# fp4 feed-forward: fp16 halves split in SBUF and turned by DMA transposes instead of TensorE transposes

## The reference

```
x = x + 0.5 * L0_ffn(layernorm(x));  x = x + L0_attn(layernorm(x));  x = x + 0.5 * L0_ffn(layernorm(x))
x = x + 0.5 * L1_ffn(x);             x = x + L1_attn(layernorm(x));  x = x + 0.5 * L1_ffn(x)
```

```
def fp4_quant_dequant(x):               # blocks of 16 along the last dim
    scale = maximum(max(abs(xb)) / 6, 1e-12)
    return GRID[searchsorted(MID, abs(xb / scale))] * sign(xb) * scale      # GRID = 0 .5 1 1.5 2 3 4 6
def fp4_linear(x, w): return einsum('bsk,nk->bsn', fp4_quant_dequant(x), fp4_quant_dequant(w))
h = silu(fp4_linear(x, w_gate)) * fp4_linear(x, w_up)                       # w: (704, 256)
return fp4_linear(h, w_down)                                                # w_down: (256, 704)
```

## Time and profile before

| | us |
|---|---|
| median of three runs | 2584.41 |
| span of the profiled execution, the only time that the page gives for it | 2581.7 |
| PE busy | 2337.3 |
| DVE busy | 1892.3 |
| ACT busy | 1681.8 |
| POOL busy | 880.3 |

### The profile page before, as it was taken

How to read it: one execution, slowest core, us unless ns; L and a number is a source line. 1 busy time by engine, 2 the same in 40 slices (tenths; PEclk the granted TensorE clock), 3 DMA queues, 4 the chain that set the end, 5 groups by cost and what they waited for, 6 DMA issues and landing times.

```text
span 2581.7 us, 54517 instructions
## 1 busy us (share of the span) xinstructions
PE 2337.3 (91%) x22748; PEld 1779.9 (69%) x22748; DVE 1892.3 (73%) x3201; ACT 1681.8 (65%) x2940; POOL 880.3 (34%) x631
## 2 busy tenths in 40 slices
PE   2889989888999998999898989989898989999999
PEld 2556666666777776777676767667676768777788
DVE  8788889997896887777878777668777774542631
ACT  4476666555757684776757575757767586675666
POOL 1222122212413221363536344453626264132122
PEclk9899999998999998999999999999999999999999
DMA  5000000000000000000000000000000000000000
GB/s 177 19 1 1 1 1 1 1 1 1 1 1 1 1 1 26 2 18 10 14 14 14 14 4 24 2 26 2 14 22 14 22 2 10 9 1 9 9 10 9
DMA packets 34981, 33.08 MB, mean 13 GB/s; under 512 B 7664, under 2 KB 34096, under 8 KB 34736
## 3 DMA queue, kind: packets, MB, share of 16 engines
q1 hardware_dynamic: 34736, 29.60, 3.5%
HBM read 12.54 MB, written 4.19 MB: 6 GB/s over the span
## 4 chain that ended last, share of the span: by engine, by line
PE 67%; DVE 18%; ACT 7%; issue 4%; POOL 2%; SPq 1%; DMA 1%; DVEq 0%; ACTq 0%
PE psum L747 17%; PE psum L749 16%; PE psum L748 16%; PE psum L753 6%; PE psum L1174 2%; PE psum L1176 2%; PE psum L1025 2%; PE psum L1175 2%; PE psum L1078 2%; DVE a1pr L1939 1%; PE psum L1055 1%; ACT a1PT L1481 1%; DVE a1nm L1916 1%; POOL a1pr L2177 1%; SPq L722 1%
## 5 line engine op out<-in xcount | busy, mean ns | idle before, releaser
L2190 POOL TENSOR_TENSOR f1hT<-f1g,f1hT 128x512 f16<-128x512 f32 x256 | 306.6, 1202 | 641.3 <-ACT f1hT L1584 640.5
L2177 POOL TENSOR_TENSOR a1pr<-a1PT,a1pr 128x1024 f16<-128x1024 f32 (+1 forms) x176 | 360.7, 2051 | 293.4 <-DVE a1pr L1939 293.3
L747 PE MATMUL psum<-f1sl,f1w1h 128*128 128x256 f16 x1024 | 285.1, 278 | 9.8 <-ACT f1g L1579 7.7
L747 PE MATMUL psum<-f1w2h,f1hT 128*128 128x256 f16 x1024 | 281.4, 275 | 6.1 <-issue 3.9
L748 PE MATMUL psum<-f1sl,f1w1h 128*128 128x256 f16 x1024 | 284.6, 278 | 0.0
L749 PE MATMUL psum<-f1sl,f1w1l 128*128 128x256 f16 x1024 | 284.3, 278 | 0.0
L748 PE MATMUL psum<-f1w2l,f1hT 128*128 128x256 f16 x1024 | 280.5, 274 | 0.0
L749 PE MATMUL psum<-f1w2h,f1hT 128*128 128x256 f16 x1024 | 280.4, 274 | 0.0
L1916 DVE TENSOR_REDUCE a1nm<-psum 128x2 f32<-128x768 f32 (+3 forms) x176 | 197.9, 1124 | 59.5 <-PE psum L1005 58.4
L1939 DVE CAST a1pr<-a1PT 128x1024 f16<-128x1024 f32 (+1 forms) x176 | 173.6, 988 | 77.6 <-ACT a1PT L1481 64.0
L2166 POOL TENSOR_TENSOR f0h<-f0Y,f0sc 128x704 f32<-128x704 f32 x64 | 91.4, 1428 | 326.4 <-DVE f0Y L1786 326.3
(11 more groups left out here) (344 smaller groups left out, 6904.1 us busy)
## 6 DMA issues: line engine op xcount, KB each, us to landing
a1Q<-a1st SPq DMA_DIRECT2D x96, 64.0 KB, 2.6
a1K<-a1st SPq DMA_DIRECT2D x96, 64.0 KB, 2.6
x<-in_L_attn_x SPq DMA_DIRECT2D x8, 512.0 KB, 8.0
out<-x SPq DMA_DIRECT2D x8, 512.0 KB, 3.0
wslot<-in_L_ffn_w SPq DMA_DIRECT2D x1, 1024.0 KB, 8.7
wraw<-in_L_ffn_w SPq DMA_DIRECT2D x1, 1024.0 KB, 5.9
wslot<-in_L_ffn_slot_embeds SPq DMA_DIRECT2D x1, 1024.0 KB, 8.2
a1Q<-a1mr SPq DMA_DIRECT2D x64, 4.0 KB, 1.7
```

The lines of the kernel that those rows point to most:

```text
L747: e.matmul(out, lh, rh, start=start, stop=False)
L2177: e.tensor_tensor(a1["pr"][:, i % 2, 1, :, 0:w], a1["PT"][:, i % 2, :, 0:w], a1["pr"][:, i % 2, 0, :, 0:w], ALU.subtract).then_inc(s["a1_pl"])
L2190: e.tensor_tensor(hT1[:, c % 2, 1, 2 * hp:2 * hp + 2, :], gg[:, hp % 2, :, :], hT1[:, c % 2, 0, 2 * hp:2 * hp + 2, :], ALU.subtract).then_ ...
```

## The change

The fp4 feed-forward no longer uses PE to turn its operands.

- The halves are split before turning. For tokens ACT copies f0xh to fp16 and DVE subtracts the low half, one instruction each per pair. For inner values ACT copies f0h to fp16 (704 columns) and POOL subtracts the low half (704 columns); the product L2166 stays on POOL ahead of both. The halves live in the memory of f0Mx and f0M, read as fp16 (names xhl and hhl).
- SP issues DMA transposes from these into f0xT (four per pair of tiles, 128x256 fp16 each, 64 KB) and f0hT (two per tile, 128x768 fp16 each, 192 KB).
- The scaling by XS and HS that sat in the PSUM copies moves into the constants of the scale computation (1/6 becomes XS/6 or HS/6, and so on).
- The last 64 inner values are no longer doubled: the sixth block has them in its first 64 rows, and the weights' rows 64 to 127 of it are set to zero, after a copy of the upper rows to the lower ones.
- Waits follow: Abs into f0Mx and f0M waits for the transposes that read the buffer before, the gate products wait for f0_x0 or f0_x1, the down products for f0_h0 or f0_h1. The planner gets an entry for the transposing DMA, and orders all engines anew.

The diff, without the lists of semaphore names and of generators, the constants of the inner values' scales, and unchanged lines:

```diff
@@ -262,6 +262,9 @@
...
         return self.vec(out)
+
+    def dma_start_transpose(self, out, src):
+        return self.note(60, None, 2.0 * out.shape[0] * self.each(out))
@@ -571,11 +574,14 @@
...
               "scx": sb("f0scx", [P, 2, 2 * D // 16], f32, stA), "xT": sb("f0xT", [P, 2, 2, 2, 2 * P], f16, stA),
-              "h": sb("f0h", [P, 3, F], f32, stA), "Y": sb("f0Y", [P, 2, FC * P], f32, stA), "M": sb("f0M", [P, 2, F], f32, stA),
+              "h": sb("f0h", [P, 3, F], f32, stA), "Y": sb("f0Y", [P, 2, FC * P], f32, stA), "M": sb("f0M", [P, 2, FC * P], f32, stA),
               "sc": sb("f0sc", [P, 2, 2, F // 16], f32, stA), "hT": sb("f0hT", [P, 2, 2, FC * P], f16, stA),
...
+
+        xhl = f0["Mx"][:, :].bitcast(f16).rearrange("p (m i d) -> p m i d", m=2, i=2)
+        hhl = f0["M"][:, :, :].rearrange("p i n -> p (i n)").bitcast(f16).rearrange("p (i n) -> p i n", i=2)
@@ -730,11 +736,35 @@
...
+            def f0_tokens(f):
+                S = at_f0(f)
+                for tp in range(2):
+                    yield S + 7.0 + 20.0 * tp
+                    q.wait_ge("f0_xl", 2 * f + tp + 1)
+                    if f > 0:
+                        q.wait_ge("f0_u", 4 * (f - 1) + 2 * tp + 2)
+                    for i in range(2):
+                        for m in range(2):
+                            e.dma_start_transpose(f0["xT"][:, tp, m, :, i * P:(i + 1) * P], xhl[:, m, i, :]).then_inc(s[f"f0_x{tp}"], 16)
+
+            def f0_hidden(f):
+                S = at_f0(f)
+                for t in range(NT):
+                    ft = 4 * f + t
+                    yield S + 10.0 + 10.0 * t + 14.6
+                    q.wait_ge("w_k", 4)
+                    q.wait_ge("f0_hl", ft + 1)
+                    q.wait_ge("f0_dn", ft - 1)
+                    for m in range(2):
+                        e.dma_start_transpose(f0["hT"][:, t % 2, m, :].rearrange("p (c n) -> p c n", c=FC),
+                                              hhl[:, t % 2, m * F:m * F + FC * P]).then_inc(s[f"f0_h{t % 2}"], 16)
+
             def last():
...
-            return [weights(), *[chain(z, B) for z in (load, a1_moves, store)], last()]
+            return [weights(), *[chain(z, B) for z in (load, a1_moves, store)],
+                    *[chain(z, 2 * B) for z in (f0_tokens, f0_hidden)], last()]
@@ -804,21 +834,6 @@
...
-            def f0_tokens(f):
-                S = at_f0(f)
-                for tp in range(2):
-                    yield S + 7.0 + 20.0 * tp
-                    q.wait_ge("f0_xq", 2 * f + tp + 1)
-                    if f > 0:
-                        q.wait_ge("f0_u", 4 * (f - 1) + 2 * tp + 2)
-                    v = bank(0)
-                    for k in range(2):
-                        for i in range(2):
-                            o = (2 * k + i) * P
-                            ins = tr(v[:, o:o + P], f0["xh"][:, i, k * P:(k + 1) * P])
-                    ins.then_inc(s["f0_xT"])
-                    banks.after(0, "f0_xl", 2 * f + tp + 1)
-
             def f0_gate(f):
@@ -831,8 +846,7 @@
...
                             q.wait_ge("w_l", W_L["tail", 1])
-                            q.wait_ge("f0_xl", 2 * f + t // 2 + 1)
-                            q.wait_ge("f0_hT", 2 * (ft - 2))
+                            q.wait_ge(f"f0_x{t // 2}", 64 * (f + 1))
                         v = bank(n)[:, 0:FH]
@@ -852,22 +866,12 @@
...
                     hT = f0["hT"][:, t % 2, :, :]
-                    for p, cs in enumerate(((0, 1, 2, 3), (4, 5))):
-                        yield G + 14.3 + 0.6 * p
-                        q.wait_ge("f0_hq", ft + 1)
-                        v = bank(2 + p)
-                        for c in cs:
-                            o = min(c * P, F - P)
-                            ins = tr(v[:, (c - 4 * p) * P:(c - 4 * p + 1) * P], f0["h"][:, ft % 3, o:o + P])
-                        ins.then_inc(s["f0_hT"])
-                        banks.after(2 + p, "f0_hl", 2 * ft + p + 1)
                     for c in range(FC):
...
                             yield G + 18.2 + 0.3 * c
-                        if c in (0, 4):
-                            q.wait_ge("w_k", 4)
-                            q.wait_ge("f0_hl", 2 * ft + c // 4 + 1)
                         if c == 0:
+                            q.wait_ge("w_k", 8)
+                            q.wait_ge(f"f0_h{t % 2}", 32 * (ft // 2 + 1))
                             v = bank(2)[:, 0:D]
@@ -1332,17 +1336,17 @@
...
                     q.wait_ge("ln_rs", 2 * (f + 1))
-                    q.wait_ge("f0_xT", n)
+                    q.wait_ge("f0_xl", n)
                     for i in range(2):
...
                     q.wait_ge("f0_xm", n + 1)
+                    q.wait_ge("f0_x1", 64 * f)
+                    q.wait_ge("f0_x0", 64 * (f + tp))
                     e.activation(f0["Mx"][:, :], f0["Yx"][:, :], ACT.Abs, scale=MAGIC).then_inc(s["f0_xr"])
-                    yield S + 7.8 + 20.0 * tp
-                    q.wait_ge("f0_xT", n + 1)
-                    if f > 0:
-                        q.wait_ge("f0_u", 4 * (f - 1) + 2 * tp + 2)
-                    e.activation(f0["xT"][:, tp, 0, :, :], psum[:, 0, :].rearrange("p (k n) -> p k n", k=2), ACT.Copy, scale=XS).then_inc(s["f0_xh"])
+                    yield S + 6.2 + 20.0 * tp
+                    q.wait_ge("f0_xq", n + 1)
+                    e.activation(xhl[:, 0, :, :], f0["xh"][:, :, :], ACT.Copy).then_inc(s["f0_xh"])
@@ -1351,26 +1355,22 @@
...
                     q.wait_ge("f0_g", ft + 1)
-                    if ft >= 3:
-                        q.wait_ge("f0_hT", 2 * (ft - 2))
+                    q.wait_ge("f0_hl", ft - 2)
                     e.activation(f0["h"][:, ft % 3, :].rearrange("p (i n) -> p i n", i=2), psum[:, 0:2, 0:FH], ACT.Silu,
...
                     q.wait_ge("f0_hm", ft + 1)
-                    e.activation(f0["M"][:, t % 2, :], f0["Y"][:, t % 2, 0:F], ACT.Abs, scale=MAGIC).then_inc(s["f0_hr"])
+                    q.wait_ge(f"f0_h{t % 2}", 32 * (ft // 2))
+                    e.activation(f0["M"][:, t % 2, 0:F], f0["Y"][:, t % 2, 0:F], ACT.Abs, scale=MAGIC).then_inc(s["f0_hr"])
...
                     G = S + 10.0 + 10.0 * t
-                    for p in range(2):
-                        cs = slice(4 * P * p, 4 * P * p + (4 * P, 2 * P)[p])
-                        n = cs.stop - cs.start
-                        yield G + 15.3 + 1.2 * p
-                        q.wait_ge("f0_hT", 2 * ft + p + 1)
-                        q.wait_ge("f0_dn", ft - 1)
-                        e.activation(f0["hT"][:, t % 2, 0, cs], psum[:, 2 + p, 0:n], ACT.Copy, scale=HS).then_inc(s["f0_hh"])
+                    yield G + 12.8
+                    q.wait_ge("f0_hq", ft + 1)
+                    e.activation(hhl[:, t % 2, 0:F], f0["h"][:, ft % 3, :], ACT.Copy).then_inc(s["f0_hh"])
@@ -1602,6 +1602,8 @@
...
                 e.tensor_copy(idb[:, :], cst[:, C_ID:C_ID + P]).then_inc(s["w_k"])
+                for i in range(2):
+                    e.memset(hhl[:, i, 2 * F:2 * FC * P], 0.0).then_inc(s["w_k"])
@@ -1648,8 +1650,12 @@
...
                         q.wait_ge("w_l", W_L[key])
-                        e.memset(wd[0][0:64, FC - 1, :], 0.0).then_inc(s["w_k"])
-                        e.memset(wd[1][0:64, FC - 1, :], 0.0).then_inc(s["w_k"])
+                        q.wait_ge("w_k", 4)
+                        for m in range(2):
+                            e.tensor_copy(wd[m][0:64, FC - 1, :], wd[m][64:128, FC - 1, :]).then_inc(s["w_k"])
+                        q.wait_ge("w_k", 6)
+                        for m in range(2):
+                            e.memset(wd[m][64:128, FC - 1, :], 0.0).then_inc(s["w_k"])
@@ -1733,24 +1739,22 @@
...
                     q.wait_ge("f0_xn", 2 * n + 2)
-                    q.wait_ge("f0_xq", n)
+                    q.wait_ge("f0_xl", n)
                     e.tensor_reduce(c_, blocks16(v), AX, ALU.max, apply_absolute_value=True).then_inc(s["dve"])
                     q.wait_ge("dve", q.tick())
-                    e.tensor_scalar(c_, c_, 1.0 / 6.0, 1e-12, ALU.mult, ALU.max).then_inc(s["dve"])
+                    e.tensor_scalar(c_, c_, XS / 6.0, XS * 1e-12, ALU.mult, ALU.max).then_inc(s["dve"])
                     q.wait_ge("dve", q.tick())
...
                     q.wait_ge("dve", q.tick())
-                    e.scalar_tensor_tensor(blocks16(Yx), blocks16(v), -TIE, bc(r_, 16), ALU.mult, ALU.mult).then_inc(s["f0_xm"])
+                    e.scalar_tensor_tensor(blocks16(Yx), blocks16(v), -TIE * XS, bc(r_, 16), ALU.mult, ALU.mult).then_inc(s["f0_xm"])
                     yield S + 4.6 + 20.0 * tp
...
                     e.scalar_tensor_tensor(Yx, Mx, MAGIC, Yx, ALU.max, ALU.subtract).then_inc(s["f0_xy"])
-                    yield S + 8.4 + 20.0 * tp
+                    yield S + 6.6 + 20.0 * tp
                     q.wait_ge("f0_xh", n + 1)
-                    xT = f0["xT"][:, tp, :, :, :]
```

(33 more changed lines are left out.)

## The result

The changed kernel took 2605.7 us (median of four runs, 2604.3 to 2612.9) against 2582.4 of the kernel before on the same chip: a ratio of 1.0092, 95% interval 1.0076 to 1.0107, slower by 0.9%. The forecast was 2560.

The account below looks back on a forecast made before the run. PE's own work was taken as the bound. Span: 2581.7 - 56.3 (transposes) - 13.6 (POOL waits) + 38 (late data) + 8 (start and end) = 2557.8 us; forecast 2560, its own range 2538 to 2586, overall range 2520 to 2720.

Parts of the forecast that it names:

- Bound by PE: Whole kernel: PE's own work sets the end, busy 2337 of 2581.7 us, with handovers to DVE here and there.
- Removed from PE, 56.3 us: Feed-forward on PE: 512 fp32 transposes go, 0.11 us each, all 56.3 us counted as gain.
- Waits for POOL, 13.6 us: PE from 100 to 980 us: its waits for the POOL products vanish, 8.9 and 4.7 us, 13.6 us gained.
- DVE, ACT, POOL without terms: Other engines: DVE net -69.5 us, ACT net -12, POOL +104 hidden as throughput; all counted at nothing.
- The new path, 8.0 us for a tile of inner values: POOL product to first down matmul: 8.0 us, 4.1 us longer, with 4.5 us for the pair of DMAs.
- SP, "about 2.4 us of 14.2": SP's queue: 2 issues per tile and 4 more per pair take about 2.4 us of each 14.2 us tile.
- "The token transposes ... free.": Token DMAs before the gate products: asked for one half f ahead, so free except at start and end.
- the two ends: Token transposes at 55 us and 978 us: no other tile beside them, so 2 x 4 = 8 us lost.
- "I let half of each delay reach PE: 38 us.": Down products: data 1.2 us later than the order assumes, half reaching PE on 64 tiles, 38 us lost.
- The order, no term: All engines' newly planned order: no cost or gain entered in the sum for other work.
- Rival 2: First down matmul of each tile: transposes land late, PE stands there; 204 us lost, 2726 us; chance 0.31.
- Rival 3: DMA stream is the bound: pieces run one after another, 20.8 against 14.2 us per tile, +422 us, 3000 us; chance 0.05.

Follow-up runs that it names:

- a_merge: Changed kernel with one transposing DMA per pair of token tiles and one per tile of inner values, booked at 1250 ns, planned anew: 2514.1 us.
- t_both: Changed kernel in the stored order of the kernel before, with removed pieces taken out and the new ones fitted in: 2919.9 us.
- g_unmerge: Changed kernel's own code, four and two transposing DMAs, in exactly the order of a_merge: 2522.5 us.
- h_cost: Changed kernel with only the inner values by DMA, tokens still turned on PE, planned anew at 1250 ns per transposing DMA: 2573.6 us.
- x_cost: Changed kernel with only the tokens by DMA, inner values still turned on PE, planned anew at 1250 ns per transposing DMA: 2611.4 us.
- t_h: Changed kernel with only the inner values by DMA, tokens still turned on PE, in the adapted order of the kernel before: 2804.0 us.
- t_x: Changed kernel with only the tokens by DMA, inner values still turned on PE, in the adapted order of the kernel before: 2755.3 us.

## Why the prediction was wrong

The sign was wrong, 2560 for 2606; on the spans, 2557.8 for 2603.0, 45.2 us. These 45.2 us are 21.8 that PE did not save (34.5 for 56.3), 18.3 more behind the silu and 30.0 spread over PE's other idle time, less 24.9 by which the waits on the tiles of the change grew less than forecast (7.5 for 38 + 8 - 13.6 = 32.4). So the terms that the forecast had for waiting were too large, not too small; what failed is what it had at nothing. Step by step, in its order:

- **Bound by PE.** Right: 88% of the span is still PE, and the chain is PE 58%.
- **Removed from PE, 56.3 us.** Right as work (62.9 us in a_merge at nearly the clock of before), 34.5 us in the changed kernel, with a granted clock of 0.955 for 0.971 and PE's idle time at 300 for 244 us (t_both: 549 us and 0.916; small differences don't follow, g_unmerge has 250 us and 0.976). The forecast had no term for that; it is 22 us.
- **Waits for POOL, 13.6 us.** Gone as said, but silu, for which PE waited 1.3 us before, has 19.6.
- **DVE, ACT, POOL without terms.** Right. POOL's subtraction takes 1614 ns (forecast 1.63 us), its busy time grew by 92 us, and no wait of PE names it.
- **The new path, 8.0 us for a tile of inner values.** Right to 0.1 us at its shortest; the pair lands 4.1 us after the first issue (forecast 4.5).
- **SP, "about 2.4 us of 14.2".** Wrong by a factor of two: 2 x 1.29 + 2 x 1.25 = 5.1 us per tile. Four for a pair of token tiles hold the queue for 5.0 us and land 6.2 us after the first starts.
- **"The token transposes ... free."** Wrong, though not by all of the 32.1 us: behind 100 us it is 20.6 for 6.9 before, over the whole span 32.1 for 22.6, 9.5 us more, where the forecast had 8 us for the two ends. Asking for them one half ahead holds for the buffer that they write, not for the data that they read, which depend on a chain of their own, nor for f0Mx, of which there is one: ACT's Abs into it waits 16.8 us for these DMAs, in five waits.
- **"I let half of each delay reach PE: 38 us."** Mis-sized. It was added to a span that held 17.6 us of such waits already; the changed kernel has 26.1 us for f0hT, 8.5 more. The data come 0.8 us later than booked (4.1 for 3.3), not 1.2, and there is no fixed share: the waits on f0hT are 180 us in the order of before (t_both) and 9.0 in an order made for the inner values alone (h_cost).
- **The order, no term.** The step that failed, and it decided the sign. The forecast took the new order to be as good as the old one for all other work. Orders of the same code spread over 52 us (changed) and 24 us (before), and over 83 us with a_merge's; the one that the changed kernel got is the worst of the six that the planner made for its code, and two others with nothing but a constant of the planner moved are faster than before. Two parts of it can be told apart: booked at 60 ns for 1.25 us, the order takes 38 us longer until the last down product than with the right price (means of three), and 15.2 of the 21.3 us that the span grew stand behind that product, by the luck of the order (11.1 of them are work that moved there). The mean of the changed kernel over three orders, 2577, is within the forecast's own range of 2538 to 2586 and 11 us under the mean of before, which three orders can't tell from nothing.
- **Rival 2** gave the slower side, for another reason: its condition, a pair of 5.3 us or more, didn't hold, and PE waited at 15 down products of 64.

What stays open is why one order has 25 us less of waiting behind the last down product than another; it lies in the softmax attention and the slots, whose instructions are the same, and no run took it apart. Open too is why PE waits longer for silu in the planned orders with the inner values' DMAs (19.6 us, 16.7 in a_merge, 14.0 in h_cost, for 1.3 before and 3.9 in x_cost).

## What to carry to other kernels

Where a planner writes the order anew, one build before and one after measure the planner's luck as much as the change: build three orders of each before believing 1%, and compare them up to the last instruction that was changed as well as over the whole. Give the planner the true cost of the new instruction. Take the waits that a change brings less those that it removes before blaming the largest. A longer path in an order made for a shorter one can cost far more than the room in the old trace lets expect (t_h: 218 us lost, 49 us of room missing), so price such a change only together with a new order. A transposing DMA holds its queue by the DMA, hardly by the byte, so few large ones are safer where the order is not made for many: merging gained 48 us in the order with the wrong price, 8 us in one with the right one.

## What the runs showed of the hardware

- A transposing DMA holds SP's queue for 1.25 us (64 KB) and 1.29 us (192 KB); merged ones 1.23 us (256 KB) and 1.43 (384 KB). Direct ones took about 0.6.
- It lands 2.4, 2.8, 3.1 and 3.7 us after its issue for these sizes, at 64 KB as soon as a direct one (2.6). 384 KB hold 12 blocks of 128x128, so ten blocks more than 64 KB take 1.3 us more. Rival 3 is out. The Trainium skill (VectorE: DVE Perf Modes, The three transpose paths) has 1309 ns for 128x128 bf16; taken as a rate that would be an estimate of 15.7 us for the 12 blocks, and the trace rules it out. By the Trainium skill's 261 GB/s for a transposing DMA (DMA: Bandwidth & Descriptors, Latency and other measured facts) the 384 KB would take 1.5 us, an estimate, which the trace allows.
- The mean granted clock is lower where PE stands idle for longer: 0.971 in the kernel before (244 us idle), 0.955 changed (300), 0.941 in t_x (383), 0.935 in t_h (433), 0.916 in t_both (549). PE is busy 2337 us before and, with 512 transposes fewer, 2367 us in t_both, where a down product's matmul takes 348 ns at the median for 273.
